# VectorE reads the one-hot's column numbers and the message bias from PSUM instead of SBUF, in a graph network kernel

## What is computed

```
# layer 0
msg = relu((x[src] * edge_weight) @ W_msg + b_msg)
agg = segment_sum(msg, dst)
x   = layernorm(x + relu(agg @ W_out + b_out))
# layers 1 and 2, with their own weights
xt  = einsum('nd,rde->rne', x, W)          # 8 relations
agg = segment_sum(xt[edge_type, src], dst)
y   = relu(agg + x @ SW + b)
# at the end
x   = layernorm(x + y of layer 2)
```

## Time and profile before

| | |
|---|---|
| median of 3 runs | 7509.95 us |
| span of the profiled execution, first to last instruction | 6622.7 us |
| median less span (no total is given for the profiled execution itself) | 887.3 us |
| POOL busy | 4948.3 us, 75% |
| PE busy | 3199.1 us, 48% |
| DVE busy | 1746.3 us, 26% |
| ACT busy | 686.1 us, 10% |
| granted PE clock, mean | 0.58 of full speed |
| mean busy share of the 16 DMA engines, by queue | 19.1% POOL's, 6.0% SP's and ACT's |

### The profile page before, as it was taken

The page is one execution under the profiler, slowest core; times in us unless marked ns, Lnnn a source line. Parts: engine busy times, 40 slices in busy tenths (PEclk is TensorE's granted clock), DMA queues, the critical chain, the costliest instruction groups (busy, mean ns, idle before and its releaser), DMA issues. The chain is left out here.

```text
span 6622.7 us, 52372 instructions
## 1 busy us (share of the span) xinstructions
PE 3199.1 (48%) x12124; PEld 2491.7 (38%) x12124; DVE 1746.3 (26%) x4136; ACT 686.1 (10%) x2063; POOL 4948.3 (75%) x5004
## 2 busy tenths in 40 slices
PE   4455555555555444444445544443444444443443
PEld 4344444444444333333333333333333333333333
DVE  3344444444444311111111111111111111111112
ACT  1112222222222100000000000000000000000000
POOL 4777777777777677777777777767777777777776
PEclk7566666656666656666665666665555555555555
DMA  4122222222222222222222222221222222222222
GB/s 130 52 80 83 83 83 83 83 83 83 83 83 87 76 54 76 76 75 75 75 72 76 76 75 76 76 77 50 56 57 58 58 58 57 57 57 56 58 57 55
DMA packets 255517, 474.23 MB, mean 72 GB/s; under 512 B 90635, under 2 KB 143412, under 8 KB 255454
## 3 DMA queue, kind: packets, MB, share of 16 engines
q0 software_dynamic: 159744, 327.48, 19.1%
q1 hardware_dynamic: 92620, 144.65, 6.0%
q10 hardware_dynamic: 3090, 1.38, 0.1%
HBM read 351.16 MB, written 121.98 MB: 71 GB/s over the span
## 5 line engine op out<-in xcount | busy, mean ns | idle before, releaser
L576 POOL DMA_INDIRECT rows<-rel_table,index x3328 | 3306.4, 994 | 1070.0 <-issue 1009.7
L622 PE MATMUL bank<-onehot,rows 128*128 128x128 f32 x9984 | 2337.4, 408 | 3369.7 <-DMA rows<-rel_table,index 2340.9
L622 PEld LDWEIGHTS bank<-onehot,rows 128*128 128x128 f32 x9984 | 2024.6, 301 | 3668.2 <-DMA rows<-rel_table,index 1590.4
L576 POOL DMA_INDIRECT rows<-msg_table,index x1664 | 1629.8, 979 | 587.6 <-issue 583.3
L608 DVE TENSOR_TENSOR agg<-agg,bank 128x128 f32 x624 | 179.5, 288 | 3569.0 <-PE bank L622 3540.5
L596 DVE SCALAR_TENSOR_TENSOR rows<-rows,weight,bm 128x128 f32<-128x128 f32 x1664 | 474.6, 347 | 1146.8 <-DMA rows<-msg_table,index 1146.8
L584 DVE TENSOR_TENSOR onehot<-columns,place 128x1024 f32<-128x1024 f32 x624 | 765.8, 1227 | 19.6 <-issue 9.7
L819 PE MATMUL bank<-wr,feat 128*128 128x512 f32 x784 | 641.8, 969 | 3.5 <-ACT feat L767 2.4
L568 ACT ACTIVATE rows<-rows 128x512 f32<-128x512 f32 x416 | 261.8, 629 | 1657.9 <-DVE rows L596 1657.9
L819 PEld LDWEIGHTS bank<-wr,feat 128*128 128x128 f32 x784 | 236.9, 332 | 198.8 <-issue 194.6
L559 ACT ACTIVATE index<-rel_index 128x8 int32 (+1 forms) x416 | 85.4, 207 | 1546.4 <-DMA rows<-rel_table,index 1542.3
(11 more groups left out here) (65 smaller groups left out, 628.6 us busy)
## 6 DMA issues: line engine op xcount, KB each, us to landing
rel_table<-tab SPq DMA_DIRECT2D x196, 512.0 KB, 2.7
rows<-rel_table,index POOLq DMA_INDIRECT x3328, 2.5
rows<-msg_table,index POOLq DMA_INDIRECT x1664, 2.5
x_dram<-normed SPq DMA_DIRECT2D x98, 64.0 KB, 2.9
xin<-x_dram SPq DMA_DIRECT2D x98, 64.0 KB, 2.0
xin<-in_x_dram SPq DMA_DIRECT2D x97, 64.0 KB, 2.4
out_dram<-normed SPq DMA_DIRECT2D x97, 64.0 KB, 2.0
tab<-in_x_dram SPq DMA_DIRECT2D x24, 256.0 KB, 2.8
```

What stands on the lines that cost most here:

```text
L576: nc.gpsimd.indirect_dma_start(rows[:, st.u, t, :], None, table, bass.IndirectOffsetOnAxis(ap=index[:, st.u, t:t + 1], axis=0)).then_inc(s ...
L622: ins = nc.tensor.matmul(ps_edge[k][:, 0:P], rows[:, st.u, t, :], onehot[:, k, t, :], start=t == 0, stop=t == TPG - 1)
```

## The change

Bank 5 is no longer used for the node products, which keep bank 4 alone. After the message table is made, DVE copies `columns` and `bm` into bank 5 once, and from then on L584 and L596 read them there. PE's wait ahead of L797 and L802 asks for the L849 of the block just before, since there is one bank. The message table still goes through banks 4 and 5.

```diff
-        ps_a = [bank[4], bank[5]]
+        ps_a = bank[4]
         ps_t = [bank[6], bank[7]]
+        ps_sheet = [bank[4], bank[5]]
+        ps_columns = bank[5][:, 0:P]
+        ps_bm = bank[5][:, P:P + D]
...
             nc.vector.tensor_tensor(
                 out=onehot[:, k, :, :],
-                in0=columns[:, :].unsqueeze(1).to_broadcast([P, TPG, P]),
+                in0=ps_columns.unsqueeze(1).to_broadcast([P, TPG, P]),
                 in1=group_cols(place, st, lead).rearrange("p o t -> p (o t)").unsqueeze(2)
...
                             out=rows[:, st.u, t, :], in0=rows[:, st.u, t, :],
-                            scalar=w[:, 0, t:t + 1], in1=bm[:, :], op0=ALU.mult, op1=ALU.add)
+                            scalar=w[:, 0, t:t + 1], in1=ps_bm, op0=ALU.mult, op1=ALU.add)
...
-                need(nc.tensor, sems.xuse, st.n - 1)
+                need(nc.tensor, sems.xuse, st.n)
                 if layer == 0:
-                    nc.tensor.matmul(ps_a[k][:, 0:D], sums[:, k, :], wo[:, :], start=True,
+                    nc.tensor.matmul(ps_a[:, 0:D], sums[:, k, :], wo[:, :], start=True,
                                      stop=False)
...
                 nc.vector.scalar_tensor_tensor(
-                    out=y[:, k, :], in0=ps_a[k][:, 0:D], scalar=0.0, in1=xin[:, st.u, :],
+                    out=y[:, k, :], in0=ps_a[:, 0:D], scalar=0.0, in1=xin[:, st.u, :],
...
             eng.wait_ge(s_w, WEIGHTS)
+            eng.wait_ge(msg_sems.tabd, SHEETS)
+            eng.tensor_copy(ps_columns, columns[:, :])
+            eng.tensor_copy(ps_bm, bm[:, :]).then_inc(s_spread, 1)
+            eng.wait_ge(s_spread, 1)
             layers(eng, unfit)
```

More of the change, by code:

```diff
@@ L252, in build @@
         s_zero = sem("s_zero")
+        s_spread = sem("s_spread")
         class EdgeSems:
@@ L720, in emit @@
                     need(eng, s.tst[st.u], loaded(st) - 16)
-                    eng.tensor_copy(sheet_out[0:r, st.u, :], ps_a[st.u % 2][0:r, :]
+                    eng.tensor_copy(sheet_out[0:r, st.u, :], ps_sheet[st.u % 2][0:r, :]
                                     ).then_inc(s.tabd, 1)
@@ L728, in emit @@
                     for u in range(QUAD):
-                        ins = eng.matmul(ps_a[st.u % 2][0:r, u * D:(u + 1) * D],
+                        ins = eng.matmul(ps_sheet[st.u % 2][0:r, u * D:(u + 1) * D],
                                          sheet_feat[:, st.u % 2, u * P:u * P + r], wm[:, :],
@@ L794, in pe_nodes @@
                 nc.tensor.wait_ge(sems.sums, st.n + 1)
-                need(nc.tensor, sems.xuse, st.n - 1)
+                need(nc.tensor, sems.xuse, st.n)
                 if layer == 0:
-                    nc.tensor.matmul(ps_a[k][:, 0:D], sums[:, k, :], wo[:, :], start=True,
+                    nc.tensor.matmul(ps_a[:, 0:D], sums[:, k, :], wo[:, :], start=True,
                                      stop=False)
-                    ins = nc.tensor.matmul(ps_a[k][:, 0:D], ones[0:1, :], bo[0:1, :],
+                    ins = nc.tensor.matmul(ps_a[:, 0:D], ones[0:1, :], bo[0:1, :],
                                            start=False, stop=True)
                 else:
-                    ins = nc.tensor.transpose(ps_a[k][:, 0:D], sums[:, k, :], ident[:, :])
+                    ins = nc.tensor.transpose(ps_a[:, 0:D], sums[:, k, :], ident[:, :])
                 ins.then_inc(sems.a, 1)
```

## The result

The changed kernel was **slower**, by little but clear of noise: 7557.64 us median against 7511.46 us, ratio 1.0063 (95% interval 1.0043 to 1.0084). I had forecast 7292 us, and 7222 to 7342 us as the range. The profiled execution took 7540.8 us with a span of 7539.1 us, so only 1.7 us lie outside the span, where I had carried 887 us over from the kernel before.

The account below looks back on a forecast made before the run. POOL's gathers were taken as the bound: span 6622.7 - 218.2 us of stalls + 0.5 us for the single bank = 6405.0 us, plus 887.3 us around the span, 7292 us, range 7222 to 7342 us.

Parts of the forecast that it names:

- the end of the sum: Time outside the profiled span: 887.3 us, carried over unchanged and added to the predicted span of 6405.0 us.
- POOL is never held up by the engines that eat its rows: POOL's waits: ten for a free row buffer, 3.0 us in all, so the span is POOL's sum of gathers.
- rival D: Much of the 887 us outside the span is the same stall, unseen: at most 688 us, 6822 us; chance 0.03.
- anything that shortens a gather counts in full: POOL's gathers at L576: time saved there shortens the span fully; work on DVE, ACT or PE counts for nothing.
- Step 1: One-hot L584 with columns from PSUM: removes 215.4 us of gather stalls; its own length taken as unchanged.
- step 2: Scaling L596 with bm from PSUM: removes 2.8 us of gather stalls; its length 0.29 to 0.35 us, worth nothing.
- rival C: Timed runs have more or fewer stalls than the profiled one, 171 to 288 us: 7222 to 7339 us; forecast with this 0.90.
- Step 3: Bank 4 alone for the node product, PE waiting for the previous block's L849: costs 0.5 us.
- Step 4: Two copies into PSUM and a wait ahead of the first one-hot: 0.6 us together, covered, so 0.
- Step 5: L840, DVE's remaining 2-port candidate: could hold gathers up 12.7 us; taken as 0, 12.7 kept for the range.
- B: Rival: PSUM reads make L584 and L596 much longer, DVE bounds layer 0; 7599 us at three times; chance 0.02.
- The sign that I had set for B: POOL's waits for PE's L622 of tens of us would show DVE bounding layer 0 through longer PSUM reads.

Follow-up runs that it names:

- fifth group: Runs on a fourth chip: before 7508.11 us, repeated for its trace 7513.48 us; changed kernel with bias row from SBUF 1.0049, with half of PE's group matmuls 0.994.
- third group: Runs on a third chip: before 6668.29 us; changed kernel 0.9595, with PE's node product one step later 0.9585; single bank and wait alone 0.9999.
- seven groups: The follow-up runs, each group beside its own runs of the kernel before on the same chip; before took 6556.69 us in the first, 7564.04 us in the seventh.
- lead 2: Gathers' row numbers made two groups ahead (IDX_LEAD 2), as in before; three ahead measured 0.9795 with the change and 0.981 in before.

## Why the prediction was wrong

**The step that failed** is the end of the sum: "887.3 us lie around the profiled span; nothing in the trace shows them, and I carry them over unchanged". They do not lie around the span, which is 1.7 to 1.8 us short of the time wherever both were taken. They are time inside it, in executions with spells, while the shown profile came from one without. Between the shown trace and the fifth group's trace of before the span grows by 899.5 us; POOL's idle time before gathers grows by 825.5 us of these and the gathers' own by 69.4 us. POOL's recorded waits lead back from there, through ACT and DVE, to PE's signals, which come up to 33.5 us late. The argument that POOL is never held up by the engines that eat its rows therefore held for the profiled execution and not for the timed ones. A gap of 13% between a profile and a time was a sign that the profile showed other conditions; I gave that doubt 0.03 (rival D), and filled D with the wrong content, more of the same stalls. With the delays, "anything that shortens a gather counts in full" fails as well: the gathers lost 283.5 us of busy time from the fifth group's before to the measured change, and POOL's idle time grew by 305.2 us.

**Step 1** (one-hot) and **step 2** (scaling) were right as mechanism. In the one trace of the change without spells the span is 6404.3 us; my sum said 6405.0. That close a meeting needs no luck in the stalls, since a kernel without them has the same span whatever they were before. What was off is before's own side, as rival C said: the stalls were 219 us in the shown trace and lie between 155 and 272 us by visit (busy time less 4992 medians). The gain is 265.8 us between the two spans of the third group. The Trainium skill's rule in SBUF — State Buffer, Who interferes with whom, that a VectorE instruction with two SBUF inputs holds up a GpSimd instruction that reads SBUF, agrees: with one input in PSUM the longest gather after the first is 962 ns in the third group. Its other, inferred remark, by which a tensor_tensor would not stall a gather, is refuted by the 1006 ns mean of before. Step 2's 2.8 us hold where there are no spells (2.3 to 2.7 us in the later traces); with them the scaling costs 31 us in layer 0 beside the old one-hot and 53 us without it, because DVE gets its work late and in heaps there, which the shown profile could not tell.

**Step 3** (single bank) was right: 0.9994, 0.9999 and 1.0007 in three groups, each interval around 1. **Step 4** (two copies) was right as far as seen: in the third group they take 0.29 and 0.28 us and the first one-hot starts at 90.3 us, 8.7 us ahead of the first scaling. **Step 5** (L840) was right to take 0: in the third group the longest gather is 962 ns, 17 ns over the median, and in the measured change 15 gathers lose 0.5 us to it.

**The rivals.** B came out on the measured side, slower, but by another way: L588 is at 1218 ns and L600 at 342 ns, so PSUM reads slow nothing. The sign that I had set for B, waits of POOL for PE's L626 (the old L622) of tens of us, came without B: 31.0 us, and 139.7 us more as "remote". Among my rivals nothing had the gathers freed and the time unchanged, which is what happened: POOL alone was not the bound there.

**What stays open.** Why some executions have the spells and the late signals: the seven groups' traces separate them by chip (two chips without, four with, and the first comparison was of the second kind), and no program of mine made or removed them there. But only one chip was visited twice, both times without, so chip and hour are not told apart, and the recording is an untested rival too. Within the loop of layer 0 DVE's spells bunch near the 20th, 84th, 147th and 210th instruction after the loop's branch, and near the 45th, 108th, 172nd and 235th, so about 64 apart. In layer 1 of the measured change 21 of the 61 distances between POOL's pauses are 47.3 to 47.7 us, the time of four groups (40.1 us) and one pause, two to a turn of DVE's loop (95 us). So there the delays keep step with the program's place. That may point to the supply of instructions, or to anything else that counts them; no run tried it. The Trainium skill, Runtime: NRT & Kernel Launch, Instruction fetch mechanics, says that a taken branch can force a fetch of the target and stall the engine; no run here isolates a branch. Open too is the half per cent that the PSUM inputs cost with spells. It is not the bank's wait. PE had 20 spells in both traces with SBUF inputs and lead 2, and 49 to 67 in the four with the column numbers in PSUM and all matmuls; that goes with it and does not explain it.

## What to carry to other kernels

Before a sum is made from a profile, hold its span against the timed executions: here they differ by 1.7 to 1.8 us wherever both are of one execution. Where they differ by much more, the profile is of other conditions, and a resource that bounds it may not bound them. If VectorE instructions with both inputs in SBUF hold up GpSimd's gathers, as here, one operand in PSUM can free them (up to 4.1%), and the trace tells it beforehand, by instructions of the same engine that already read PSUM. Where a second limit holds the time, shorter gathers only turn into waits; the version to run then is the one that also gives the feeding queue more lead (0.98 of before here with or without the change; on a chip without spells that lead was not tried).

## What was not expected of the hardware

- The same program took 6557 to 6668 us on two chips and 7508 to 7564 us on four others, with the granted PE clock alike (0.583 and 0.591 in two traces of before).
- In a slow spell PE, DVE and SP start one instruction per 0.7 or 1.4 us, SP for plain register work too. In the same traces PE's signal for a finished group comes up to 33.5 us after its last recorded matmul, 305 to 491 of 509 to 592 recorded signals over 1 us; those of DVE's one-hots and sums and of ACT's index tiles don't. On ACT my count finds only two short ones, before 31 us, in every trace I counted, and on POOL none.
- A gather that begins 100 to 1050 ns into a one-hot ends 0.82 us after it. One that is more than 0.1 us old when the one-hot begins is not held by it: none of 287 in the shown trace. So the gather needs what the one-hot holds only early on.
- Which share of one-hots meets a gather drifts by visit in an unchanged program: the gathers' busy time was 4867.9 and 4928.5 us on the same chip.
- With spells DVE's scalings come in rows of up to eight, and a gather can stand through a whole row, 2.43 us at most: their stalls in layer 0 went from 3 to 31 us by the spells, and to 53 us when the one-hot's were gone as well.
